# Attention with its side work in small pieces: layer norm, router choice and inverse sums on other engines

## What is computed

```python
x = x + 0.5 * ffn(layernorm(x))      # router: best of 4 groups, both its experts, weights normalised
x = x + attn(layernorm(x))
x = x + 0.5 * ffn(layernorm(x))

# attn: 16 heads of 16; windows of 128 tokens every 64 (7 a batch)
scores = einsum('bhnqd,bhnkd->bhnqk', qw, kw) * scale + pos_bias
probs  = softmax(scores)
ow     = einsum('bhnqk,bhnkd->bhnqd', probs, vw)
merged = zeros.at[:, :, idx].add(ow)  # plus the last window once more
return (merged / counts) @ Wo + bo

# ffn: h = silu(x @ gate_w[e]) * (x @ up_w[e]);  out = sum_e w[e] * (h @ down_w[e])
```

## Time and profile before

| | us |
|---|---|
| median of 3 runs | 1549.4 (1544.67 to 1550.34) |
| the profiled execution | 1547.95 |
| its span, first to last instruction | 1546.2 |
| busy: PE, DVE, ACT, POOL | 1303.2, 918.6, 646.2, 244.2 |
| mean granted TensorE clock | 0.915 |

### The profile page before, as it was taken

One profiled execution on the slowest core, in us unless ns is written; L12 is line 12 of the kernel. 1 busy time (PEld: TensorE's weight loads), 2 busy tenths in 40 slices (PEclk: granted clock), 3 DMA queues, 4 the chain that ended last, 5 costly groups with the idle time before them and its releaser, 6 DMA issues.

```text
span 1546.2 us, 33371 instructions
## 1 busy us (share of the span) xinstructions
PE 1303.2 (84%) x8771; PEld 845.9 (55%) x8772; DVE 918.6 (59%) x3765; ACT 646.2 (42%) x2339; POOL 244.2 (16%) x286
## 2 busy tenths in 40 slices
PE   4422699999996798989999899989893799999996
PEld 4411466666664455555565555555563466666664
DVE  5789444444443577777687877787864344444442
ACT  1114322223222476657466575757750122232221
POOL 3322001100011101120111212021212011000100
PEclk9999999999998699888779897989956899999998
DMA  9500442000002101010100202020106121000000
GB/s 303 207 28 28 175 151 59 17 14 14 14 15 80 45 15 49 1 49 15 35 31 9 56 9 57 1 63 2 49 15 248 52 59 55 14 14 14 15 15 14
DMA packets 51247, 81.37 MB, mean 53 GB/s; under 512 B 6912, under 2 KB 34816, under 8 KB 51136
## 3 DMA queue, kind: packets, MB, share of 16 engines
q1 hardware_dynamic: 44320, 61.29, 12.5%
q0 software_dynamic: 6816, 18.81, 3.4%
HBM read 45.81 MB, written 27.97 MB: 48 GB/s over the span
## 4 chain that ended last, share of the span: by engine, by line
PE 61%; DVE 15%; issue 8%; ACT 4%; POOL 2%; DMA 1%; DVEq 1%; SPq 1%; ACTq 0%; POOLq 0%
PE bank L807 24%; PE bank L759 9%; PE bank L825 9%; PE bank L940 6%; DVE w_all L1387 5%; PE bank L896 4%; PE bank L967 3%; DVE w_all L1397 2%; PE bank L978 2%; PE bank L923 2%; DVE hb L1226 2%; ACT sl L637 2%; ACT w_all L719 1%; PE bank L773 1%; DVE stats L1095 1%
## 5 line engine op out<-in xcount | busy, mean ns | idle before, releaser
L719 ACT ACTIVATE w_all<-w_all 128x128 f32<-128x128 f32 x896 | 347.1, 391 | 162.9 <-DVE w_all L1387 161.7
L807 PE MATMUL bank<-w_all,xt 128*128 x1680 | 390.2, 383 | 12.6 <-DVE xt L1238 3.5
L807 PEld LDWEIGHTS bank<-w_all,xt 128*128 128x128 f16 x1680 | 165.1, 98 | 197.0 <-issue 37.1
L1226 DVE SCALAR_TENSOR_TENSOR hb<-bank,ew,sl 128x512 f32<-128x512 f32 x140 | 105.2, 751 | 211.0 <-ACT sl L637 211.0
L1387 DVE CUSTOM_DVE_ANT_0 w_all<-bank,w_all 128x128 f32<-128x128 f32 x896 | 198.2, 286 | 44.7 <-PE bank L940 32.3
L825 PE MATMUL bank<-w_all,ht 128*128 x1680 | 206.2, 273 | 1.2 <-DVE yt L1251 1.2
L637 ACT ACTIVATE sl<-bank,back 128x512 f32<-128x512 f32 x140 | 95.9, 685 | 239.0 <-PE bank L807 239.0
L759 PE MATMUL bank<-ident,w_all 128*128 128x128 f32 x896 | 166.1, 316 | 22.1 <-ACT w_all L719 12.9
L1397 DVE COPY w_all<-bank 128x512 f32<-128x512 f32 x224 | 153.1, 685 | 43.3 <-PE bank L967 43.3
L825 PEld LDWEIGHTS bank<-w_all,ht 128*128 128x128 f16 x1680 | 164.2, 98 | 19.3 <-issue 1.7
L719 ACT ACTIVATION_READ_ACCUMULATOR w_all<-w_all 128x1 f32 x896 | 169.7, 189 | 0.0
(11 more groups left out here) (168 smaller groups left out, 1603.6 us busy)
## 6 DMA issues: line engine op xcount, KB each, us to landing
big<-sorted_rows SPq DMA_DIRECT2D x70, 130.5 KB, 2.1
saved<-w_all SPq DMA_DIRECT2D x16, 512.0 KB, 2.8
w_all<-saved SPq DMA_DIRECT2D x4, 2048.0 KB, 14.1
w_all<-mid SPq DMA_DIRECT2D x9, 512.0 KB, 3.7
big<-in_L_attn_hidden_states SPq DMA_DIRECT2D x8, 512.0 KB, 4.3
w_all<-in_L_ffn_gate_w SPq DMA_DIRECT2D x8, 512.0 KB, 11.2
w_all<-in_L_ffn_up_w SPq DMA_DIRECT2D x8, 512.0 KB, 10.8
w_all<-in_L_ffn_down_w SPq DMA_DIRECT2D x8, 512.0 KB, 11.3
```

The lines of the kernel that those rows point to most:

```text
L719: a = nc.scalar.activation(prob[:, u % NB, h], sbias[:, u % NB, h], ACT.Exp, bias=nmax[:, u % NB, h:h + 1], scale=-1.0, accum_out=rsum[:, ...
L807: mm = nc.tensor.matmul(bank[2 * e + w][:], xt[:, hx, c, :], flat(gu16[:, bass.ds(g * E + e, 1), w, hw, c, :]), start=(i == 0), stop=(i == ...
L1226: nc.vector.scalar_tensor_tensor(out=hb[:, e], in0=bank[2 * e + 1][:], scalar=ew[:, e:e + 1], in1=sl[:, e], op0=ALU.mult, op1=ALU.mult).th ...
```

## The change

The table `SIDE` becomes a table for each engine (with its own for the first and the last batch), and the steps become smaller. PE does half of a k or q projection at a time (`k0a`, `k0b`), the logits by tile, and of v only tile 0 of the next batch, with tiles 1 to 3 in units 1 to 3 of their own batch; v's shifts are three pairs of DMAs, each behind its tiles. The factors move to units with u % 4 == 3. POOL takes over the small steps of the layer norm, the normalising and most of the router's choice (DVE keeps the four steps of `best_groups` and the step of `place` that reads PSUM). DVE keeps the statistics, tile by tile, those of the next batch's norm now in the batch before. ACT takes over spreading the inverse. The scatter stands at the end of POOL's batch, and the next load of `stage` waits for its landing. Ahead of the first batch only v tile 0 is projected. In the tail behind batch 7, norm and choice stay on DVE.

```diff
-        SIDE = {2: ("stats0",),
-                3: ("stats1",),
-                5: ("norm0",),
-                6: ("norm1", "o0"),
-                7: ("o1", "add0"),
-                8: ("o2", "add1"),
-                9: ("o3", "add2"),
-                10: ("add3",),
-                11: ("turn_prep", "copy_prep", "r_stats0"),
-                12: ("r_stats1",),
-                13: ("k0", "copy_k0"),
-                14: ("k1", "r_norm0", "copy_k1"),
-                15: ("r_norm1",),
-                17: ("turn_route",),
-                18: ("copy_route",),
-                20: ("logits", "q0", "copy_q0"),
-                21: ("q1", "copy_q1"),
-                22: ("choose0",),
-                23: ("choose1", "v0"),
-                24: ("rank", "copy_v0"),
-                25: ("choose2", "v1"),
-                26: ("choose3", "place", "copy_v1"),
-                27: ("v2", "v3"),
-                28: ("copy_v2",),
-                29: ("copy_v3",)}
...
+        PE_SIDE = {1: ("v1",), 2: ("v2",), 3: ("v3",), 5: ("turn_prep",), 7: ("k0a",), 8: ("k0b",), 9: ("o0",),
+                   10: ("o1",), 11: ("o2",), 12: ("o3",), 13: ("k1a",), 14: ("k1b",), 15: ("q0a",), 16: ("q0b",),
+                   18: ("turn_route",), 20: ("l0",), 21: ("l1",), 22: ("l2",), 23: ("l3",), 24: ("q1a",), 25: ("q1b",),
+                   27: ("v0", "rank")}
...
+        PE_LAST = {1: ("v1",), 2: ("v2",), 3: ("v3",), 9: ("o0",), 10: ("o1",), 11: ("o2",), 12: ("o3",),
+                   18: ("turn_route",), 20: ("l0",), 21: ("l1",), 22: ("l2",), 23: ("l3",), 26: ("rank",)}
...
+        ACT_SIDE = {5: ("copy_prep",), 8: ("copy_k0",), 14: ("copy_k1",), 16: ("copy_q0",), 18: ("copy_route",),
+                    23: ("logits",), 25: ("copy_q1",)}
...
+        DVE_SIDE = {2: ("copy_v1",), 4: ("copy_v2", "copy_v3"), 10: ("add0",), 11: ("r_stat0", "add1"), 12: ("add2",),
+                    13: ("r_stat1", "add3"), 14: ("r_stat2", "r_stat3"), 20: ("stat0",), 22: ("stat1",), 24: ("best",),
+                    25: ("stat2",), 26: ("stat3",), 28: ("copy_v0",),
+                    29: ("place",)}
...
-            def shift_values(b, par):
-
-                sp.wait_ge(v_ready, b * TB + TB)
+            def shift_values(b, par, i):
+
+                sp.wait_ge(v_ready, b * TB + (i + 2))
                 v = va[par]
-                sp.dma_start(v[0:STRIDE, 1:NWIN:2], v[STRIDE:W, 0:NWIN - 1:2]).then_inc(va_shifted, 16)
-                sp.dma_start(v[STRIDE:W, 1:NWIN:2], v[0:STRIDE, 2:NWIN:2]).then_inc(va_shifted, 16)
+                n = 2 * i + 1
+                sp.dma_start(v[0:STRIDE, n], v[STRIDE:W, n - 1]).then_inc(va_shifted[i], 16)
+                sp.dma_start(v[STRIDE:W, n], v[0:STRIDE, n + 1]).then_inc(va_shifted[i], 16)
 
             def batch(b, par, first_, last):
+                shift_values(b, par, 0)
+                shift_values(b, par, 1)
+                shift_values(b, par, 2)
                 if not first_:
 
-                    sp.wait_ge(stage_free, b - 1 + OPEN)
+                    sp.wait_ge(scattered, (b - 1) * (16 * TB) + 16 * TB * B)
                     sp.dma_start(stage[:, :, 0:D], rows_of(b - 1)).then_inc(res_loaded, 16)
                 if not last:
                     sp.wait_ge(xa_ready, (prep_use(b + 1) + 1) * TB)
                     load_batch(b + 2)
-                    shift_values(b + 1, 1 - par)
...
+            def norm(k, said, n, st, src, mean, rstd):
+
+                pool.wait_ge(said, n)
+                pool.sem_inc(pool_open, 1)
+                step = Chain(p_norm, (k - (B + 1)) * PNORM_STEPS)
+                s, d, v, dd, _, var = (ln_t[:, i, :] for i in range(6))
+                pool.tensor_tensor(s, st[:, :, 1], st[:, :, 4], ALU.add)
+                pool.tensor_tensor(d, st[:, :, 1], st[:, :, 4], ALU.subtract)
+                step(pool.tensor_tensor(v, st[:, :, 2], st[:, :, 5], ALU.add))
+                pool.tensor_scalar(mean, s, 0.5, None, ALU.mult)
+                pool.tensor_scalar(d, d, 0.5, None, ALU.mult)
+                step(pool.tensor_scalar(v, v, 1.0 / D, LN_EPS, ALU.mult, ALU.add))
+                step(pool.tensor_tensor(dd, d, d, ALU.mult))
+                step(pool.tensor_tensor(var, v, dd, ALU.add))
+                assert step.n == PNORM_STEPS
+                pool.tensor_tensor(rstd, var, mhalf[:], ALU.pow).then_inc(rstd_ready, 1)
+                pool.wait_ge(rstd_ready, k + 1)
+                pool.wait_ge(xnt_psum, k * DC + OPEN)
+                pool.sem_inc(pool_open, 1)
+                for t in range(TB):
+                    pool.tensor_scalar(xa[:, t, :], src[:, t, 0:D], mean[:, t:t + 1], rstd[:, t:t + 1],
+                                       ALU.subtract, ALU.mult).then_inc(xa_ready, 1)
...
+            def choose(r, rows):
...
+                step = Chain(p_route, (r - B) * PROUTE_STEPS)
+                pool.wait_ge(eq_ready, r - B + 1)
+                pool.sem_inc(pool_open, 1)
+                step(pool.tensor_scalar(rest[:, :, 1:G], eq[:, :, 0:G - 1], -1.0, 1.0, ALU.mult, ALU.add))
+                step(pool.tensor_tensor(rest[:, :, 2], rest[:, :, 2], rest[:, :, 1], ALU.mult))
+                step(pool.tensor_tensor(rest[:, :, 3], rest[:, :, 3], rest[:, :, 2], ALU.mult))
...
+                step(pool.tensor_tensor(rc, den, minus[:], ALU.pow))
+                step(pool.tensor_tensor(rc, best[:], rc, ALU.mult))
+                step(pool.tensor_tensor(rows[:, :, C_W:C_W + E], u01[:], bc(rc, 2, [P, TB, E]), ALU.mult))
+                return step
...
+            def find_place(r, place_no, step):
+
+                pool.wait_ge(place_ready, r - B + 1)
+                pool.sem_inc(pool_open, 1)
+                step(pool.tensor_tensor(place[:], place[:], oh[:], ALU.mult))
+                step(pool.tensor_tensor(pair[:], place[:, :, 0:2], place[:, :, 2:G], ALU.add))
+                step(pool.tensor_tensor(posf[:], pair[:, :, 0], pair[:, :, 1], ALU.add))
+                pool.tensor_copy(pos[:, place_no], posf[:]).then_inc(pos_ready, 1)
...
             def batch(b, par, first_, last):
-                if not last:
-                    power(prep_use(b + 1), ln_t[:, 5, :], ln_t[:, 4, :])
                 if not first_:
 
                     pool.wait_ge(o_done, (b - 1) * TB + OPEN)
 
                     pool.sem_inc(batch_open, 1)
                 pool.memset(ctxt[par][:], 0.0).then_inc(ctx_zero, 1)
+                if not last:
+                    norm(prep_use(b + 1), stat_ready, b + 1, stats, xb, mean_b[:], ln_t[:, 4, :])
                 if not first_:
                     accumulate(b - 1, 1 - par, NWIN - 1)
                     bias_residual(b - 1)
                 for n in range(NWIN - 1):
                     accumulate(b, par, n)
                     if n == 1 and not first_:
-                        power(route_use(b - 1), ln_t[:, 5, :], stage[:, :, C_RSTD])
-                    if n == (3 if last else 4) and not first_:
-                        scatter(b + (B - 1), route_use(b - 1), stage, B, scattered[1])
+                        pool.tensor_copy(stage_i[:, :, C_TOK], token_no[:, bass.ds((b - 1) * TB, TB)]
+                                         if type(b) is not int else token_no[:, (b - 1) * TB:b * TB])
+                        norm(route_use(b - 1), r_stat_ready, b, stats_r, stage, stage[:, :, C_MEAN], stage[:, :, C_RSTD])
+                    if n == NWIN - 3 and not first_:
+                        step = choose(b + (B - 1), stage)
                 if not first_:
-                    pool.wait_ge(scattered[1], b * (16 * TB))
-                    pool.sem_inc(stage_free, 1)
+                    find_place(b + (B - 1), B, step)
+                    scatter(b + (B - 1), route_use(b - 1), stage, B)
...
+                act.wait_ge(rinv_ready, b * NWIN + (n + 1))
+                if n or type(b) is not int or b:
+
+                    act.wait_ge(rb_done, b * NWIN + n)
+                nc.scalar.activation(rexp[:], rinv.unsqueeze(2).to_broadcast([P, H, HD]), ACT.Copy,
+                                     scale=inv_count[:, n:n + 1]).then_inc(rexp_ready, 1)
...
-            def project(m, w):
-
+            def project(m, w, c):
+
+                mm = nc.tensor.matmul(bank[6 + m][:], w[:, c, m * P:(m + 1) * P], xnt[:, c, :],
+                                      start=(c == 0), stop=(c == DC - 1))
+                if c == DC - 1:
+                    mm.then_inc(proj_done, 1)
...
+            def project_v(b, t):
+
+                pe.wait_ge(wv_ready, VPERM)
+                if t == 0:
+                    pe.wait_ge(q_ready, b * DC + DC)
+                if t == 1:
+                    pe.wait_ge(v_ready, b * TB + 1)
+                if t == 2:
+                    pe.wait_ge(pos_ready, b + (B - 1))
...
-                    if u % NQ == 2:
+                    if u % NQ == 3:
...
+                if not early:
+                    dve.wait_ge(rexp_ready, b * NWIN + n)
```

(23 more changed lines are left out.)

276 lines of the change are left out of this document (151 added, 125 removed).

## The result

The changed kernel takes **1508.6 us** (median of 4 runs, 1505.3 to 1512.8) against 1549.9 for the kernel before in the same comparison: ratio 0.973, 95% interval 0.969 to 0.978. It is faster by 41 us and inside the range. The forecast was 65 us less, so 24 us of the gain are missing, and the experiments look for them. Its profiled execution took 1505.25 us, its span 1503.5 us against 1546.2.

What follows compares the result with a forecast made beforehand. PE was taken to bound the kernel, through idling and a low clock. Middle batches -62, start -3 and last batch 0 make -65: 1547.95 us profiled becomes 1483, median 1484; eight-in-ten range 1463 to 1526.

Steps and rivals of the forecast that it cites:

- rival A: Middle batches: the clock still falls once a batch, 76.0 us each, +28, giving 1512 us; chance 0.25.
- PE's wait: At the input transposes in unit 5: PE waits for POOL's normalised tiles, 0 to 2 us a batch.
- Start: Ahead of the first scores: three v tiles move back inside a batch, -3 us (0 to -4).
- Last batch: Last batch: work and idle fall to 60.4 from 71.6, but 8.0 is lost before the first output matmul; net 0.
- The middle batches: Batches 1 to 6: 65.3 work, 5.1 idle, 0.9 wait, 71.3 us each at full clock; -62 over six.
- normalising one tile on POOL: POOL's norm at the batch boundary: 0.5 us a tile, between a copy (0.29) and an add (0.73).
- the prediction's own formula: Batch boundary: PE waits 30c - 10.8 us for POOL's tiles where that exceeds 0.9, c being one small POOL step.
- Small steps on POOL: Norm and choice on POOL: 0.32 us a step with its wait, ends 0.22 and 1.04.
- Rival B: Batch boundary: POOL's small steps are dear, deciding from 0.43 us each; at 0.6 about 1578 us; chance 0.08.
- The spread: Seven inverse spreads a batch on ACT: 0.4 us each, 2.8 a batch; DVE's 1.94 us hold goes.
- A wait brings a fall: Batch boundary: dips under 2 us of idling lead to clock falls; priced at half of 9.5 us a batch.
- Rival C: Middle batches: handovers loosened by a unit halve the idle, 68.7 us a batch, 1468 us; chance 0.12.

Runs made afterwards that it cites:

- e1: Changed kernel with the normalising of the next batch's input tiles moved from POOL back to VectorE: 1508.6 us, ratio 0.974.
- e3: Changed kernel with the second half of the next batch's query projection, and ScalarE's copy of it, one unit earlier: 1512.7 us, ratio 0.979.
- e4: Changed kernel with the last batch's routing earlier (transposes, logits, rank, POOL's choice, places and scatters): 1511.5 us, ratio 0.978.
- e8: e2_norm_early with the spreading of the inverse sums moved from ScalarE back to VectorE: 1511.3 us, ratio 0.975.
- e10: Kernel with POOL's early normalising and three waits fewer, plus the last batch's logits, rank, places and scatters earlier: 1502.0 us, ratio 0.967.
- e11: e3 plus unread filler matmuls on TensorE in units 12 to 17 of the last batch: 1524.1 us, ratio 0.981.
- e9: The kernel before the change with only the spread of the inverse sums moved to ScalarE: 1539.9 us, ratio 0.993.
- e7: e2_norm_early with TensorE's small side pieces in the middle batches joined again: 1506.9 us, ratio 0.980.
- e2_norm_early: Changed kernel with POOL's norm of the next batch's input moved ahead, right behind the choice, same work: 1481.9 us, ratio 0.959.

## Why the prediction came out as it did

- **Sign and size.** Faster, at 1508.6 with 1484 forecast: what came is near rival A (1512), the clock falling once more in a batch. Of the signs named, the middle batches (77 to 79 us inside the loop, not 70 to 73), their clock (0.91 to 0.93, not 0.95) and PE's wait (2.0 to 5.1 us, not 0 to 2) came out on the wrong side.
- **Luck in the total.** 15.1 us of the gain, in batch 0 and behind the last batch, were not forecast; without them the span would have fallen by 28 of the 65. And the last batch's 9.6 came in an execution in which its clock held: in e1 and e3 the same code took 56 us, a gain of 3.
- **Start** (-3): 3.2, right. **Last batch** (0): 9.6 won, 8.6 lost at its end, right in sum, and the loss by the mechanism given (8.0 forecast; the wait of 10 us or more is 12.8). **Batch 0** was taken as unchanged and gained 7.6, as did the stretch behind the last batch (7.5, of which 5.8 behind PE's last instruction, unexplained).
- **The middle batches** (-62) gave 23.5: that is the step that fell short, by 38.5 us, and the unforecast 7.6 and 7.5 above take back some of it. (The 62 were counted from the 490.0 us of the earlier trace rows, whose first cut lies ahead of mine; between my cuts the kernel before takes 484.6, so up to 5.4 of the 38.5 may be the cut's.) Their work of 65.3 us at full clock was right: 65.6 was measured where the clock was 1.00.
- **The mis-sized term** in it is normalising one tile on POOL: 0.5 was taken between 0.29 and 0.73; it is 1.21, outside both ends. The error is of kind: the bracket held a copy and an add of two tensors, while this step takes two scalars a partition. Four tiles come 2.8 us later, all of it on the path to the transposes. From the places ready to the last tile POOL took 16.6 us (739.10 to 755.69) where the prediction has 12.9: 2.85 are the tiles, 0.85 a pause ahead of the first scatter. By the prediction's own formula, 30c - 10.8 at a pitch of 0.38 gives a wait of 0.6, with the tiles 3.4; PE waited 19.4 us in the six intervals, 3.2 a batch. Moved ahead of the scatters with the work unchanged, the norm gave back 24 us, and a batch of 72.4 against the forecast 71.3. That these 24 equal the 24 missing in the total is chance: in the middle batches alone more was missing, elsewhere 15 came unforecast. The Trainium skill, GPSIMD Engine Reference, "3.1 Elementwise — side-by-side cycle accounting", calls some 2.6 cycles an element the floor of two inputs and 1.8 the best case of a tight loop; my estimate from it would be that the one-input step is no dearer than the add of 0.73. The trace has 1.21, and the measurement decides.
- **Small steps on POOL**: 0.20 plus 0.18 of wait, a pitch of 0.38 against 0.32; 1.04 with pow. Rival B, which needed 0.43, did not come. `choose` took 7.5 us against 6.8.
- **The spread**: 0.51 us on ScalarE against 0.4. The hold of 2.29 us is gone. In the changed order of POOL the spread's return to VectorE comes with 1.6%, part of which may be the chip's; alone it gives 0.7%.
- **A wait brings a fall.** The prediction priced this in rival A at half of 9.5. Over the six intervals a batch is 461.1 / 6 = 76.9 us with PE busy 69.4: 4.1 over the work for the low clock, and 7.5 idle against 6.0. That the clock would be full was judged too likely: in the changed kernel it fell to 0.50 behind each of the five waits for the tiles, the one of 2.04 us too.
- **Rival C** (1468) had halved idling in it. With POOL's early order and three waits fewer the kernel takes 1467, its better middle batches 69.2 (68.7 forecast for C).

What stays open: why the same dip in the same code sometimes lets the clock fall and sometimes not. It moved single batches by 3 to 12 us between executions and chips, and is the reason why e3, e4, e8, e10 and e11 can't be read by their times alone. Open too: where batch 0's 7.6 us and the 7.5 behind the last batch come from, and how the edits add up; e9 and e7 price the spread (11 us) and the small pieces (25 us) in different kernels, and nothing prices the rest of the change alone.

## What to carry to other kernels

Bracket a new step by steps with the same kinds of operands; a tile step with per-partition scalars can lie outside the bracket of copies and adds. When work goes to a slower engine, ask first where in its queue it stands: here the same 32 us of POOL work a batch cost 24 us more of the kernel's time in one place than in another, and a faster engine fed just as late gained 9 us in the middle batches and nothing in the total. What the removal of a wait is worth, in a kernel whose clock falls, has to be read in the batches where the clock stayed the same; the total mixes in falls in code that the edit doesn't touch.

## What the hardware showed that I had not expected

- A TensorE that idles 1.3 to 1.5 us of a slice of 3 keeps its clock in one execution and runs at half for 17 us in another, with the same code.
- At a clock of 0.95 and of 1.00 a batch of e2_norm_early took 72.3 and 72.4 us: half speed cost nothing there, since it fell into time in which TensorE would have waited.
- The same engine step on POOL: 128x256 with two scalars a partition 1.21 us, with a second tensor 0.73, on four columns 0.20.
- Straight code for six batches took as long as the loop it replaced (1481.6 and 1481.9 us, on two chips).
